# Shifted-window attention block with MLP, one core: both bands' scores and both bands' attend put together, with fixed PSUM banks for Q, K and V

## The chip, the cores and the metric

One Trainium2 chip, one of its cores. The metric is the device time of one execution in microseconds (us): the median of 3 runs for the kernel before. One further execution was profiled; all rows below are from it.

## The reference

A Swin transformer block over x of 32 images, 56 x 56 tokens, 128 channels, all in float32, window 7 x 7 (N = 49 tokens), shift 3, 4 heads of 32 channels:

```python
h = roll(layernorm(x, g1, b1), (-3, -3))              # 64 windows an image
q, k, v = split(windows(h) @ w_qkv + b_qkv)
attn = softmax((q * 32**-0.5) @ k.T + rel_bias + MASK)    # 49 x 49 for each window and head
x = x + roll(windows_back((attn @ v) @ w_proj + b_proj), (3, 3))
h2 = layernorm(x, g2, b2)
out = x + gelu(h2 @ w_fc1 + b_fc1) @ w_fc2 + b_fc2    # 128 -> 512 -> 128
```

## The kernel before

An image is cut into 4 steps of 14 rows, so there are 128 steps in all. A step has two bands of 7 rows; a band is 8 windows side by side, 392 tokens. The tokens of a step lie as 7 tiles of 112 (`HALVES`: a first half of 4 tiles, a second of 3).

The work is a software pipeline over steps, written out by hand as one `step(at)` for each engine, and each engine runs its list strictly in the order of the code. In the iteration of step s, with `at.has(d)` standing for step s+d, there run: statistics and normalisation of the input (`xn1`) for s+2; its transposes, Q and K for s+1; V, scores, softmax and attention for s; projection, residual, second layer norm and the first seven chunks of fc1/gelu for s-1; the last chunk, fc2 and the last addition for s-2. Semaphores order the engines; `wait(..., at.count(...))` waits for so many increments.

What runs where:

- TensorE (PE): `scores` (64 matmuls a band), `make_hidden` n = 0 to 7 (fc1 for one band and one chunk, three matmuls each), `project` (7 tiles, in two halves), `make_values`, `make_out` (fc2, two halves), `transpose_probs`, `transpose_x` and `transpose_x2` (two halves each), `attend` (64 matmuls a band), `make_q`, `make_k` (band 0 in plain float32, band 1 as three products).
- ScalarE (ACT): `gelu`, `exp`, and nearly all copies out of PSUM: `copy_v0`, `copy_probsT` (two instructions a band), `copy_x`, `copy_x2`, `copy_q`, `copy_k`, `copy_o`, and `round_x`. Exp and Gelu need different tables, so two table loads stand in a step: one ahead of the first exp, one at the `table_probe` line.
- VectorE (DVE): `shift_scores` (bias, maximum, subtraction), `inverse_sums`, statistics (`raw_stats`, `mean_var`), `normalise`, additions to the stream (`add_to_stream`; `add_mlp` is the last addition of layer two), `split_x`, `split_x2`, `copy_v1`.
- GpSimd (POOL): `normalise_probs`, the two reciprocal roots (`rstd1`, `rstd2`) and two additions of a bias row to the stream (signalled by `x1_biased` and `x_biased`).
- SyncE (SP) issues all loads (they wait for `x_biased`) and all stores (they wait for `out_added`).

PSUM has 8 banks: 0 to 3 for scores and transposed probabilities (two a band), 4 and 5 for Q, K, V and O in turn, 6 and 7 for whatever is indexed by tokens. `V_USE`, `Q_USE` and `K_USE` say which of banks 4 and 5 each band uses; O of one band fills 196 columns of both, one bank for each parity of the window.

The parts of TensorE's list that the change touches, in their order before: scores 0; hidden 7; project 0 and 1; values 0; scores 1; out 0; transpose_probs 0; out 1; transpose_x 0; attend 0; transpose_x2 0; transpose_x 1; values 1; transpose_x2 1; Q 0; hidden 0; K 0; hidden 1; transpose_probs 1; hidden 2 and 3; attend 1; hidden 4; Q 1; hidden 5; K 1; hidden 6. `make_q` of band 1 waits for O of band 1 to have been copied, since it writes the same bank:

```python
wait(pe, o_copied, at.count(2, band + 1))
qk_product(at, Q_USE[band], 0, band).then_inc(qk_made, 1)
```

Of the kernel before, what the change touches and what calls it, by code (L numbers as in the profile page):

```python
# [93 lines left out]
def swin_block(nc, x, g1, b1, w_qkv, b_qkv, w_proj, b_proj, rel_slices, g2, b2, w_fc1, b_fc1, w_fc2,  # L94
# [3 lines left out]
    with ExitStack() as ctx:  # L98
# [148 lines left out]

        V_USE, Q_USE, K_USE = (0, 0), (1, 0), (0, 1)

        def qkvo_psum(use):  # L250
            return psum[:, QKVO_BANK + use % 2, :]

        def o_psum(parity):
            return psum[:, QKVO_BANK + parity, 0:PAIRS * N]

# [9 lines left out]
        def v_copy(band):  # L265
            rows = HALF + N
            return (vs[0:rows, band, :, :].rearrange("m a c -> m (a c)"),
                    qkvo_psum(V_USE[band])[0:rows, :])

# [71 lines left out]
        def _(pool):  # L341
# [16 lines left out]

            def step(at):
                if at.has():  # L360
                    normalise_probs(at, 0)
# [11 lines left out]
                if at.has(2):  # L373

                    wait(pool, var1_ready, at.count(1, 1, 2))
                    pool.tensor_tensor(rstd1[:, :], ve1[:, :], minus_half[:, :], ALU.pow).then_inc(rstd1_ready, 1)  # L376
                if at.has(1):

                    wait(pool, x_loaded[at.slot(1)], dma_count(at.slot(1), at.image(1)))
                    wait(pool, xn1_ready, at.count(2, 2, 1))  # L380

                    if at.has(1 - STEPS):
                        wait(pool, out_stored[at.slot(1)], dma_count(at.slot(1), at.image(1 - STEPS)))
                    pool.tensor_tensor(stream[:, at.slot(1), :, :], x_in[:, at.slot(1), :, :],  # L384
                                       brow_proj[:, :].unsqueeze(1).to_broadcast([TOK, TILES, C]),
                                       ALU.add).then_inc(x_biased, 1)

# [3 lines left out]
        def _(act):  # L391
# [10 lines left out]

            def copy_probsT(at, band):
                for f in range(2):
                    wait(act, probsT_made, at.count(4, 2 * band + f + 1))
                    act.activation(probsT[:, band, f, :, :, :].rearrange("p a q n -> p (a q n)"),  # L406
                                   psum[:, S_BANK + 2 * band + f, :], ACT.Copy).then_inc(probsT_copied, 1)

            def copy_o(at, band):

                wait(act, o_made, at.count(2, band + 1))
                image = oT[:, :, band, :].rearrange("c i (a w j) -> c w a i j", w=2, j=WIN)
# [28 lines left out]
            def copy_q(at, band):  # L441
                wait(act, qk_made, at.count(4, 2 * band + 1, 1))
                for parity in range(2):
                    last = act.activation(qd[:, band, parity, :], qkvo_psum(Q_USE[band])[:, 0:BAND], ACT.Identity,  # L444
                                          bias=bias_q[:, parity:parity + 1], scale=parity_one[:, parity:parity + 1])
                last.then_inc(qk_copied, 1)

            def copy_k(at, band):
                wait(act, qk_made, at.count(4, 2 * band + 2, 1))
                act.activation(kT[:, band, :], qkvo_psum(K_USE[band])[:, 0:BAND], ACT.Identity,  # L450
                               bias=bias_k[:, :]).then_inc(qk_copied, 1)
# [11 lines left out]
            def step(at):  # L463
# [7 lines left out]
                if at.has(1):  # L471
                    copy_x(at, 0)
                if at.has():
                    copy_o(at, 0)
                if at.has(-1):
# [23 lines left out]
                if at.has():  # L499
                    copy_o(at, 1)  # L500
                if at.has(-1):
# [13 lines left out]
        def _(dve):  # L515
# [130 lines left out]
            def step(at):  # L646
# [58 lines left out]
        def _(pe):  # L705
# [34 lines left out]
            def transpose_probs(at, band):  # L740

                wait(pe, probs_normed, at.count(2, band + 1))
                for f in range(2):
                    for pair in range(PAIRS):
                        last = pe.transpose(psum[:, S_BANK + 2 * band + f, 128 * pair:128 * (pair + 1)],  # L745
                                            probs[:, band, f, 2 * pair:2 * pair + 2, :].rearrange("p w m -> p (w m)"),
                                            ident[:, :])
                    last.then_inc(probsT_made, 1)

            def attend(at, band):  # L750
                wait(pe, probsT_copied, at.count(4, 2 * band + 2))

                wait(pe, (v0_copied, v1_copied)[band], at.count(1, 1))

                if band == 0:
                    wait(pe, qk_copied, at.count(4, 4))
                elif at.has(1):
                    wait(pe, qk_copied, at.count(4, 2, 1))
                pe.sem_inc(attend_begun, 1)
                for pair in range(PAIRS):  # L760
                    for parity in range(2):
                        keys = slice(HALF * parity, HALF * parity + N)
                        for h in range(HEADS):
                            rows = slice(HD * h, HD * (h + 1))
                            last = pe.matmul(o_psum(parity)[rows, pair * N:(pair + 1) * N], vs[keys, band, pair, rows],
                                             probsT[keys, band, h // 2, pair, h % 2, 0:N], start=True, stop=True)
                last.then_inc(o_made, 1)
# [6 lines left out]

            def qk_product(at, use, part, band):
                if band == 0:

                    return pe.matmul(qkvo_psum(use)[:, 0:BAND], wqk[:, part, :], xT[:, at.slot(1) % 2, 0, :, 0:N],
                                     start=True, stop=True)
                return product(qkvo_psum(use)[:, 0:BAND], wqk_hi[:, part, :], wqk_lo[:, part, :],  # L780
                               xT_hi[:, :], xT_lo[:, :])

            def make_q(at, band):

                if band == 0:
                    wait(pe, xT_copied, at.count(2, 2, 1))
                else:
                    wait(pe, xT_split, at.count(1, 1, 1))

                wait(pe, o_copied, at.count(2, band + 1))  # L790
                qk_product(at, Q_USE[band], 0, band).then_inc(qk_made, 1)

            def make_k(at, band):

                if band == 0:
                    wait(pe, v1_copied, at.count(1, 1))
                else:
                    wait(pe, o_copied, at.count(2, 2))
                qk_product(at, K_USE[band], 1, band).then_inc(qk_made, 1)

            def make_values(at, band):

                if band == 0:
                    wait(pe, qk_copied, at.count(4, 3))
                else:
                    wait(pe, o_copied, at.count(2, 1))
                rows = HALF + N
                for pair in range(PAIRS):
                    windows = xT[:, at.slot() % 2, band, 2 * pair:2 * pair + 2, :].rearrange("c w n -> c (w n)")
                    last = pe.matmul(qkvo_psum(V_USE[band])[0:rows, pair * C:(pair + 1) * C], windows[:, 0:rows],  # L810
                                     wv[:, :], start=True, stop=True)
# [58 lines left out]
            def step(at):  # L870
                if at.has():
                    scores(at, 0)
                if at.has(-2):

                    make_hidden(at, 7, -2)
                if at.has(-1):

                    wait(pe, o_copied, at.count(2, 2, -1))
# [19 lines left out]
                if at.has(1):  # L898
                    transpose_x(at, 1)
                if at.has():  # L900
                    make_values(at, 1)
                if at.has(-1):
                    transpose_x2(at, 1)
# [13 lines left out]
                if at.has():  # L917
                    attend(at, 1)
                if at.has(-1):
# [70 lines left out]
```

## Time and profile before

| | |
|---|---|
| median of 3 runs | 3276.6 us (3276.32 to 3279.51) |
| the profiled execution | 3275.45 us, its span 3273.7 us |
| granted TensorE clock, mean | 0.999 of full |
| PE busy (matmul) | 3117.6 us, 95% |
| DVE busy | 2814.3 us, 86% |
| ACT busy | 2283.0 us, 70% |
| POOL busy | 1316.7 us, 40% |
| DMA | 111.95 MB, mean 34 GB/s |

The busy shares are averages over a loop that repeats 128 times. Matmuls are pipelined, so a busy TensorE is not one at its peak; the distance from the start of one group to the start of the next says more than the duration of one. With several engines near their limit, the question is which wait ends last at each hand-over inside one step.

### The profile page before, as it was taken

The page shows a single profiled execution, that of the slowest core. Times are in us where ns is not written, and L with a number is a line of the kernel's source. Part 1 is how long each engine was busy: PE and PEld are TensorE (multiplying, and loading weights), DVE is VectorE, ACT ScalarE, POOL GpSimd, SP SyncE. Part 2 cuts the span into 40 slices and gives each one's busy share as a digit, 9 for nine tenths or more (in the row PEclk, how much of TensorE's full clock was granted, in tenths as well). Part 3 has the DMA queues.
Part 4 walks back from the last instruction along what each step waited for, and adds up shares of the span by engine and source line. Part 5 has one row for each costly group of instructions (what it writes and reads, how often), then busy time and mean ns, then how long its engine had stood idle before and what let it go on. Part 6 is the DMA issues. An engine that isn't in the chain of part 4 may idle for free.

```text
span 3273.7 us, 121784 instructions
## 1 busy us (share of the span) xinstructions
PE 3117.6 (95%) x51984; PEld 2750.4 (84%) x51984; DVE 2814.3 (86%) x7463; ACT 2283.0 (70%) x4478; POOL 1316.7 (40%) x775
## 2 busy tenths in 40 slices
PE   5999999999999999999999999999999999999998
PEld 4888888888888888888888888888888888888887
DVE  6888888888888888888888888888888888888885
ACT  3667766776777677767776777677767776776675
POOL 2344434443444444344434443444344434443442
PEclk9999999999999999999999999999999999999999
DMA  1111111111111111111111111111111111111110
GB/s 51 34 32 37 36 33 32 37 37 32 32 36 37 32 34 35 37 32 36 33 37 32 36 32 37 32 37 32 37 32 37 34 35 32 37 34 34 32 27 22
DMA packets 217584, 111.95 MB, mean 34 GB/s; under 512 B 15094, under 2 KB 216790, under 8 KB 217046
## 3 DMA queue, kind: packets, MB, share of 16 engines
q1 hardware_dynamic: 216899, 104.14, 12.4%
q8 instruction: 413, 6.77, 0.9%
q14 instruction: 125, 1.02, 0.1%
q10 hardware_dynamic: 147, 0.02, 0.0%
HBM read 52.73 MB, written 51.38 MB: 32 GB/s over the span
## 4 chain that ended last, share of the span: by engine, by line
DVE 43%; ACT 30%; PE 16%; issue 10%; SPq 0%; POOL 0%; DMA 0%; DVEq 0%; POOLq 0%; ACTq 0%
DVE stream L620 9%; DVE scores L600 8%; DVE row_max L603 8%; ACT hT L460 7%; DVE xn L588 6%; DVE raw L566 5%; ACT L482 5%; ACT qd L444 4%; PE psum L771 4%; ACT probsT L406 4%; PE psum L729 4%; DVE row_sum L613 4%; PE psum L773 3%; PE psum L772 3%; ACT xT L425 2%
## 5 line engine op out<-in xcount | busy, mean ns | idle before, releaser
L858 PE MATMUL psum<-wfc,hT 128*112 128x128 f32 x7168 | 835.6, 274 | 1.0 <-ACT hT L460 0.7
L858 PEld LDWEIGHTS psum<-wfc,hT 128*112 128x112 f32 x7168 | 797.8, 177 | 8.3 <-ACT hT L460 1.0
L356 POOL TENSOR_TENSOR probs<-probs,row_inv 128x784 f32<-128x784 f32 x256 | 389.4, 1521 | 987.1 <-DVE row_inv L615 987.1
L460 ACT ACTIVATE hT<-psum,bias_h 128x392 f32<-128x392 f32 x1024 | 598.8, 605 | 71.1 <-PE psum L773 70.7
L406 ACT ACTIVATE probsT<-psum 128x512 f32<-128x512 f32 x512 | 281.5, 613 | 484.7 <-PE psum L745 484.7
L588 DVE TENSOR_SCALAR xn<-x_in,mean,rstd 112x128 f32<-112x128 f32 x896 | 466.0, 587 | 1.8 <-POOL rstd L376 1.7
L368 POOL TENSOR_TENSOR stream<-stream,brow_fc 112x896 f32<-112x896 f32 x128 | 267.3, 2088 | 485.6 <-DVE xn L588 485.6
L771 PE MATMUL psum<-x2T_hi,wfc_hi 128*128 128x392 f32 x1024 | 448.7, 438 | 2.6 <-DVE x2T_lo L638 1.5
L400 ACT ACTIVATE probs<-scores 128x784 f32<-128x784 f32 x256 | 224.0, 875 | 210.0 <-DVE scores L605 210.0
L444 ACT ACTIVATE qd<-psum,bias_q,parity_one 128x392 f32<-128x392 f32 x512 | 318.4, 674 | 59.0 <-PE psum L773 55.8
L773 PE MATMUL psum<-x2T_lo,wfc_hi 128*128 128x392 f32 x1024 | 348.5, 340 | 0.0
L772 PE MATMUL psum<-x2T_hi,wfc_lo 128*128 128x392 f32 x1024 | 347.9, 340 | 0.0
L376 POOL TENSOR_TENSOR rstd<-ve,minus_half 112x7 f32<-112x7 f32 x128 | 190.7, 1490 | 360.7 <-DVE ve L582 360.7
L600 DVE TENSOR_TENSOR scores<-psum,bias_rel 128x784 f32<-128x784 f32 x256 | 248.9, 972 | 92.7 <-PE psum L729 92.5
L620 DVE TENSOR_TENSOR stream<-psum,stream 112x512 f32<-112x512 f32 (+1 forms) x512 | 304.5, 615 | 20.9 <-PE psum L858 13.1
L736 PE MATMUL psum<-ident,xn 112*128 112x112 f32 x1792 | 269.1, 267 | 54.4 <-DVE stream L620 41.2
L771 PEld LDWEIGHTS psum<-x2T_hi,wfc_hi 128*128 128x128 f32 x1024 | 191.8, 187 | 138.9 <-DVE x2T_lo L638 76.2
L384 POOL TENSOR_TENSOR stream<-x_in,brow_proj 112x896 f32<-112x896 f32 x128 | 286.7, 2239 | 0.0
L745 PE MATMUL psum<-ident,probs 128*128 128x128 f32 x2048 | 267.1, 274 | 9.1 <-POOL probs L356 9.1
L736 PEld LDWEIGHTS psum<-ident,xn 112*128 112x128 f32 x1792 | 177.8, 141 | 106.4 <-issue 90.0
L810 PE MATMUL psum<-wv,xT 128*113 128x128 f32 x2048 | 266.2, 273 | 0.3 <-ACT oT L414 0.3
L605 DVE TENSOR_TENSOR scores<-scores,row_max 128x784 f32<-128x784 f32 x256 | 249.5, 975 | 8.7
(78 smaller groups left out, 5869.6 us busy)
## 6 DMA issues: line engine op xcount, KB each, us to landing
x_in<-in_x SPq DMA_DIRECT2D x224, 168.0 KB
out<-stream SPq DMA_DIRECT2D x224, 168.0 KB
x_in<-in_x SPq DMA_DIRECT2D x224, 17.5 KB
out<-stream SPq DMA_DIRECT2D x224, 17.5 KB
x_in<-in_x SPq DMA_DIRECT2D x224, 10.5 KB
out<-stream SPq DMA_DIRECT2D x224, 10.5 KB
x_in<-in_x SPq DMA_DIRECT2D x32, 96.0 KB
out<-stream SPq DMA_DIRECT2D x32, 96.0 KB
```

The costliest lines, as they stand in the source:

```text
L356: pool.tensor_tensor(p, p, r.unsqueeze(2).to_broadcast([128, 2 * WINDOWS, N]), ALU.mult).then_inc(probs_normed, 1)
L406: act.activation(probsT[:, band, f, :, :, :].rearrange("p a q n -> p (a q n)"), psum[:, S_BANK + 2 * band + f, :], ACT.Copy).then_inc(prob ...
L444: last = act.activation(qd[:, band, parity, :], qkvo_psum(Q_USE[band])[:, 0:BAND], ACT.Identity, bias=bias_q[:, parity:parity + 1], scale= ...
L460: act.activation(hT[:, chunk, band * BAND:(band + 1) * BAND], tok_psum(FC1 + n)[:, 0:BAND], ACT.Gelu, bias=bias_h[:, chunk:chunk + 1]).the ...
L588: last = dve.tensor_scalar(dst[:, t, :], src[:, t, :], mean[:, t:t + 1], rstd[:, t:t + 1], ALU.subtract, ALU.mult)
L600: dve.tensor_tensor(sc, scores_psum(band), bias_rel[:, last_band, :, :, :].rearrange("p f w m -> p f (w m)"), ALU.add).then_inc(scores_bia ...
L620: return dve.tensor_tensor(s, tok_psum(use)[0:TOK, 0:(t1 - t0) * C], s, ALU.add)
L736: last = pe.transpose(tok_psum(use)[:, (t - t0) * TOK:(t - t0 + 1) * TOK], src[:, t, :], ident[0:TOK, 0:TOK])
L771: pe.matmul(made, w_hi, x_hi, start=True, stop=False)
L772: pe.matmul(made, w_lo, x_hi, start=False, stop=False)
L773: return pe.matmul(made, w_hi, x_lo, start=False, stop=True)
L858: last = pe.matmul(tok_psum(FC2 + h)[0:TOK, (t - t0) * C:(t - t0 + 1) * C], hT[:, chunk, t * TOK:(t + 1) * TOK], wfc2[:, chunk, :], start= ...
```

## The change

- PE runs the scores of both bands at the head of the step, hidden 7 and the projections behind them.
- PE runs `attend` once, for both bands (128 matmuls), where attend 1 stood. O of both bands lies in the same two banks (392 columns each), and `copy_o` runs once, with two instructions of 392 columns where there were four of 196.
- Values 1 moves up, between transpose_x 0 and transpose_x 1; transpose_x2 0 and 1 stand together behind transpose_x 1.
- Q has bank 4, K has bank 5, V has 4 for band 0 and 5 for band 1; the waits follow.
- DVE's two `add_mlp` stand together, ahead of the normalisation of `xn2`.
- POOL's addition `x_biased` for s+1 moves from the end of an iteration to its beginning.
- `transpose_probs` reads 113 partitions in place of 128, and `copy_probsT` copies 4 x 113 columns in place of 512.

```diff
-        V_USE, Q_USE, K_USE = (0, 0), (1, 0), (0, 1)
+        V_BANK, Q_BANK, K_BANK = (0, 1), 0, 1
         def o_psum(parity):
-            return psum[:, QKVO_BANK + parity, 0:PAIRS * N]
+            return psum[:, QKVO_BANK + parity, 0:BANDS * PAIRS * N]
@@ gpsimd step
+                if at.has(1):
+                    wait(pool, x_loaded[at.slot(1)], dma_count(at.slot(1), at.image(1)))
+                    wait(pool, xn1_ready, at.count(2, 2, 1))
+                    if at.has(1 - STEPS):
+                        wait(pool, out_stored[at.slot(1)], dma_count(at.slot(1), at.image(1 - STEPS)))
+                    pool.tensor_tensor(stream[:, at.slot(1), :, :], x_in[:, at.slot(1), :, :],
+                                       brow_proj[:, :].unsqueeze(1).to_broadcast([TOK, TILES, C]),
+                                       ALU.add).then_inc(x_biased, 1)
                 if at.has():
                     normalise_probs(at, 0)
...
@@ scalar
-                act.activation(probsT[:, band, f, :, :, :].rearrange("p a q n -> p (a q n)"),
-                               psum[:, S_BANK + 2 * band + f, :], ACT.Copy).then_inc(probsT_copied, 1)
+                act.activation(probsT[:, band, f, :, :, :].rearrange("p a q n -> p a (q n)")[:, :, 0:rows],
+                               psum[:, S_BANK + 2 * band + f, :].rearrange("p (a n) -> p a n", a=PAIRS)[:, :, 0:rows],
+                               ACT.Copy).then_inc(probsT_copied, 1)
-            def copy_o(at, band):
-                wait(act, o_made, at.count(2, band + 1))
+            def copy_o(at):
+                wait(act, o_made, at.count(1, 1))
...
@@ vector step
                 if at.has(-2):
                     add_mlp(at, 0)
+                    add_mlp(at, 1)
                 if at.has(-1):
                     wait(dve, rstd2_ready, at.count(1, 1, -1))
                     wait(dve, x2T_made, at.count(2, 2, -2))
                     normalise(xn2, stream[:, at.slot(-1), :, :], mean2, rstd2, xn2_ready)
-                if at.has(-2):
-                    add_mlp(at, 1)
@@ tensor
-            def attend(at, band):
-                wait(pe, probsT_copied, at.count(4, 2 * band + 2))
-                wait(pe, (v0_copied, v1_copied)[band], at.count(1, 1))
-                if band == 0:
-                    wait(pe, qk_copied, at.count(4, 4))
-                elif at.has(1):
-                    wait(pe, qk_copied, at.count(4, 2, 1))
+            def attend(at):
+                wait(pe, probsT_copied, at.count(4, 4))
+                wait(pe, v0_copied, at.count(1, 1))
+                wait(pe, v1_copied, at.count(1, 1))
+                if at.has(1):
+                    wait(pe, qk_copied, at.count(4, 2, 1))
...
             def make_q(at, band):
                 if band == 0:
                     wait(pe, xT_copied, at.count(2, 2, 1))
+                    wait(pe, v0_copied, at.count(1, 1))
                 else:
                     wait(pe, xT_split, at.count(1, 1, 1))
-                wait(pe, o_copied, at.count(2, band + 1))
+                    wait(pe, o_copied, at.count(1, 1))
@@ tensor step
                 if at.has():
                     scores(at, 0)
+                    scores(at, 1)
                 if at.has(-2):
                     make_hidden(at, 7, -2)
                 if at.has(-1):
                     project(at, 0)
                     project(at, 1)
                 if at.has():
                     make_values(at, 0)
-                    scores(at, 1)
...
                 if at.has(1):
                     transpose_x(at, 0)
                 if at.has():
-                    attend(at, 0)
+                    make_values(at, 1)
+                if at.has(1):
+                    transpose_x(at, 1)
                 if at.has(-1):
                     transpose_x2(at, 0)
-                if at.has(1):
-                    transpose_x(at, 1)
-                if at.has():
-                    make_values(at, 1)
-                if at.has(-1):
                     transpose_x2(at, 1)
...
                 if at.has():
-                    attend(at, 1)
+                    attend(at)
```

## Rows read from the trace of the kernel before

**Rows 1.** Windows, one step: length, then busy time (instructions) of each engine.

```profile
1513.03:1538.16 25.13, 24.27 (x408) 21.43 (x407) 21.91 (x60) 17.85 (x36) 10.28 (x6) 1.00 0.13 34
```

**Rows 2.** Timeline, PE, that step: start us, length us, line, operation [idle before, releaser].

```profile
1513.03 0.95 PE L729 MATMUL psum<-kT,qd 64*49 64x49 f32 x64
1513.91 0.44 PE L771 MATMUL psum<-x2T_hi,wfc_hi 128*128 128x392 f32 x1
...
1525.17 0.57 PE L736 MATMUL psum<-ident,xn 112*128 112x112 f32 x4
1525.68 0.81 PE L765 MATMUL psum<-probsT,vs 49*32 49x49 f32 x64
1526.53 0.57 PE L736 MATMUL psum<-ident,xn 112*128 112x112 f32 x4
1527.43 0.48 PE L736 MATMUL psum<-ident,xn 112*128 112x112 f32 x3 [0.32 <-DVE stream L620]
1527.74 1.04 PE L810 MATMUL psum<-wv,xT 128*113 128x128 f32 x8
1528.62 0.47 PE L736 MATMUL psum<-ident,xn 112*128 112x112 f32 x3
...
1534.01 0.80 PE L765 MATMUL psum<-probsT,vs 49*32 49x49 f32 x64 [0.26 <-ACT probsT L406]
...
1535.84 0.42 PE L771 MATMUL psum<-xT_hi,wqk_hi 128*128 128x392 f32 x1 [0.23 <-ACT oT L414]
...
1538.16 0.95 PE L729 MATMUL psum<-kT,qd 64*49 64x49 f32 x64
```

**Rows 3.** Timeline, ACT, same step.

```profile
1514.75 0.59 ACT L460 ACTIVATE hT<-psum,bias_h 128x392 f32<-128x392 f32 x1 [0.54 <-PE psum L773]
1515.36 1.28 ACT L400 ACT_TABLE_LOAD   x1
1517.07 0.87 ACT L400 ACTIVATE probs<-scores 128x784 f32<-128x784 f32 x1 [0.43 <-DVE scores L605]
...
1527.94 0.52 ACT L425 ACTIVATE xT<-psum 128x168 f32<-128x168 f32 x2 [0.26 <-PE psum L736]
...
1532.75 1.11 ACT L406 ACTIVATE probsT<-psum 128x512 f32<-128x512 f32 x2
...
1535.06 0.63 ACT L414 ACTIVATE oT<-psum 128x196 f32<-128x196 f32 x2
...
1538.27 0.59 ACT L450 ACTIVATE kT<-psum,bias_k 128x392 f32<-128x392 f32 x1
```

**Rows 4.** Timeline, DVE, same step and the head of the next.

```profile
1518.02 0.96 DVE L613 TENSOR_REDUCE row_sum<-probs 128x16 f32<-128x784 f32 x1
...
1524.34 0.68 DVE L620 TENSOR_TENSOR stream<-psum,stream 112x512 f32<-112x512 f32 x1
1524.94 1.88 DVE L588 TENSOR_SCALAR xn<-stream,mean,rstd 112x128 f32<-112x128 f32 x7
1526.73 0.55 DVE L620 TENSOR_TENSOR stream<-psum,stream 112x384 f32<-112x384 f32 x1
...
1534.80 3.67 DVE L588 TENSOR_SCALAR xn<-x_in,mean,rstd 112x128 f32<-112x128 f32 x7
1539.17 0.97 DVE L600 TENSOR_TENSOR scores<-psum,bias_rel 128x784 f32<-128x784 f32 x1 [0.71 <-PE psum L729]
```

**Rows 5.** Timeline, POOL, same step: the addition that signals x_biased.

```profile
1534.60 2.25 POOL L384 TENSOR_TENSOR stream<-x_in,brow_proj 112x896 f32<-112x896 f32 x1
```

**Rows 6.** Groups by line and form: busy us, mean ns, idle before.

```profile
L406 ACT ACTIVATE probsT<-psum 128x512 f32<-128x512 f32 x512 | 281.5, 613 | 484.7 <-PE psum L745 484.7
L414 ACT ACTIVATE oT<-psum 128x196 f32<-128x196 f32 x512 | 154.5, 380 | 18.0 <-PE psum L765 1.4
```

**Rows 7.** Timeline, SP's queue: the stores of one step.

```profile
1527.31 2.25 SPq L310 DMA_DIRECT2D out<-stream  x6
```

**Rows 8.** Windows: as rows 1, then clock, DMA share, GB/s.

```profile
1530.50:1531.50 1.00, 1.00 (x5) 0.59 (x4) 1.00 (x5) 1.00 (x3) 0.00 (x0) 1.00 0.05 13
```

More of the change, by code:

```diff
@@ L267, in v_copy @@
             return (vs[0:rows, band, :, :].rearrange("m a c -> m (a c)"),
-                    qkvo_psum(V_USE[band])[0:rows, :])
+                    qkvo_psum(V_BANK[band])[0:rows, :])
         def token_pieces(s, dram, img, tile):
@@ L443, in copy_q @@
                 for parity in range(2):
-                    last = act.activation(qd[:, band, parity, :], qkvo_psum(Q_USE[band])[:, 0:BAND], ACT.Identity,
+                    last = act.activation(qd[:, band, parity, :], qkvo_psum(Q_BANK)[:, 0:BAND], ACT.Identity,
                                           bias=bias_q[:, parity:parity + 1], scale=parity_one[:, parity:parity + 1])
@@ L758, in attend @@
                     wait(pe, qk_copied, at.count(4, 2, 1))
                 pe.sem_inc(attend_begun, 1)
[L760 to L766, printed above, removed]
+                for band in range(BANDS):
+                    for pair in range(PAIRS):
+                        cols = slice((band * PAIRS + pair) * N, (band * PAIRS + pair + 1) * N)
+                        for parity in range(2):
+                            keys = slice(HALF * parity, HALF * parity + N)
+                            for h in range(HEADS):
+                                rows = slice(HD * h, HD * (h + 1))
+                                last = pe.matmul(o_psum(parity)[rows, cols], vs[keys, band, pair, rows],
+                                                 probsT[keys, band, h // 2, pair, h % 2, 0:N], start=True, stop=True)
@@ L773, in product, with qk_product @@
                 return pe.matmul(made, w_hi, x_lo, start=False, stop=True)
-            def qk_product(at, use, part, band):
+            def qk_product(at, bank, part, band):
                 if band == 0:
-                    return pe.matmul(qkvo_psum(use)[:, 0:BAND], wqk[:, part, :], xT[:, at.slot(1) % 2, 0, :, 0:N],
+                    return pe.matmul(qkvo_psum(bank)[:, 0:BAND], wqk[:, part, :], xT[:, at.slot(1) % 2, 0, :, 0:N],
                                      start=True, stop=True)
-                return product(qkvo_psum(use)[:, 0:BAND], wqk_hi[:, part, :], wqk_lo[:, part, :],
+                return product(qkvo_psum(bank)[:, 0:BAND], wqk_hi[:, part, :], wqk_lo[:, part, :],
                                xT_hi[:, :], xT_lo[:, :])
@@ L797, in make_k @@
                 else:
-                    wait(pe, o_copied, at.count(2, 2))
-                qk_product(at, K_USE[band], 1, band).then_inc(qk_made, 1)
+                    wait(pe, o_copied, at.count(1, 1))
+                qk_product(at, K_BANK, 1, band).then_inc(qk_made, 1)
             def make_values(at, band):
[L803 to L806, printed above, removed]
+                wait(pe, qk_copied, at.count(4, 3 + band))
                 rows = HALF + N
@@ L809, in make_values @@
                     windows = xT[:, at.slot() % 2, band, 2 * pair:2 * pair + 2, :].rearrange("c w n -> c (w n)")
-                    last = pe.matmul(qkvo_psum(V_USE[band])[0:rows, pair * C:(pair + 1) * C], windows[:, 0:rows],
+                    last = pe.matmul(qkvo_psum(V_BANK[band])[0:rows, pair * C:(pair + 1) * C], windows[:, 0:rows],
                                      wv[:, :], start=True, stop=True)
@@ L876, in step @@
                 if at.has(-1):
-                    wait(pe, o_copied, at.count(2, 2, -1))
+                    wait(pe, o_copied, at.count(1, 1, -1))
                     project(at, 0)
```

30 lines of the change are left out of this document (11 added, 19 removed).

## The prediction

> **What bounds the kernel now.** I read the page first (PE 95% busy, DVE 86%, ACT 70%, POOL 40%), then a window of one step, then the chain of waits in order of time, and last the timeline of each engine over that step. The loop is strictly periodic. From the first scores of one step to those of the next are 25.13 us [rows 1, 2], and 128 such steps make 3216.6 of the span of 3273.7 us; prologue and epilogue are the other 57. So one question decides: by how much does the period change, times 128.
>
> No single engine sets the period. PE has only 0.81 us of marked idle time in a step: 0.32 ahead of the second half of transpose_x, 0.26 ahead of attend 1, 0.23 ahead of Q 1 [rows 2]. The other 24.32 us are its own work, a floor that the change does not lower, since it removes no matmul. DVE waits 0.71 us for the first scores of the next step [rows 4]. The chain of waits shows one loop through three engines, and the reader should follow it, for the sum is made along it. In times relative to the step's first scores (1513.03 is 0.00):
>
> - DVE shifts scores 0 (starts 1.02 after them), adds the projection, and takes the sums of band 0 at 4.99, just after exp 0 ended at 4.91 [rows 3, 4]. It works on without a gap to add_mlp 0 (11.31), xn2 (11.91) and add_mlp 1 (13.70, ends 14.25) [rows 4].
> - That addition releases transpose_x 1 on PE (14.40), that copy_x 1 on ACT (14.91), and behind it stands the table load for Gelu (15.43) [rows 2, 3].
> - ACT then has no idle time up to the end of copy_o 1: probsT 1 at 19.72, copy_o 1 from 22.03 to 22.66 [rows 3].
> - That releases Q 1 on PE (22.81), and from Q 1 through hidden 5, K 1 and hidden 6 it is 2.32 us to the next scores at 25.13 [rows 2].
>
> A thing saved beside this loop is worth nothing; each delay on it is paid 128 times.
>
> **The change part by part.**
>
> *Attend for both bands at the end.* PE's total is the same, but 64 matmuls that ran at 12.65, off the loop, now stand between probsT 1 and copy_o, on it. A band takes 0.85 us by the distance to the next group at the first place; at the second its row says 0.80 [rows 2]. Before, copy_o 1 started 1.05 after attend 1, and ACT came to it without idle time. With 128 matmuls the end comes 0.84 (the distance from attend 0 until ACT could copy, which its 0.85 of work makes a lower bound) plus 0.85 after the start, 1.69. Addition: 1.69 - 1.05 = +0.64; bounds 0.60 and 0.68, the doubt being a few hundredths at each end. ACT could use that time, but its list has nothing that it may take: copy_o stands behind gelu 3, and gelu 4 and everything else stand behind copy_o. On PE only hidden 4 stands between attend and Q 1, so PE waits as well.
>
> *copy_o for both bands.* Before, two instructions of 196 columns took 0.63 us and Q 1 began 0.15 later. The 392-column copy is not in the trace. 512 columns take 613 ns and 196 take 380 [rows 6], so 0.74 ns a column, and 392 take about 525 ns. Two of them, overlapping as before (0.63 against 2 x 0.38, 0.13 saved), take 0.92: +0.29. Bounds: +0.25 if the short copies' cost is mostly fixed, +0.33. The copy_o 0 that disappears (0.57 us, at about 13.5) saves nothing on the loop: ACT waits 0.26 us for copy_x 1 right behind that place [rows 3], and it will wait there again.
>
> *probsT with 452 columns.* 60 columns fewer by 0.74 are 0.04 us an instruction, two of them on the loop; -0.1 with what the clipped pattern saves at the end, bounds -0.12 and 0. The transposes of 113 partitions save nothing that I count.
>
> *Both scores at the head.* Scores take 0.88 us of PE (1513.03 to 1513.91) [rows 2]. Scores 1 moves ahead of hidden 7, so hidden 7 is 0.88 later, and so is gelu 7, which started at 1.72. Queued behind gelu 7 on ACT is the table load, and behind that exp 0. gelu 7 to table load is 0.61, the load 1.28 [rows 3]. Exp 0 can then start at 1.72 + 0.88 + 0.61 + 1.28 = 4.49 in place of 4.04, since only 0.43 of the 0.88 was idle time ahead of exp 0 [rows 3]. The sums of band 0 on DVE follow exp 0 by less than 0.1, so DVE is 0.42 late from there on, through the second shift to add_mlp 0. That DVE list has no idle time to give it back. Bounds: 0 and 0.47.
>
> *Projections 0.88 later.* Hidden 7 starts at 1.76 and takes about 0.58 (a quarter of the 2.32 above); the 14 instructions of the projections, by the 0.88 that values 1 takes for 8, take 1.5. So the first half is done at about 3.2 and the second at 3.9, and DVE, through with the first shift at 3.9, adds them at 3.9 and 4.5. Covered; it would cost what they are late. Values 0 keeps its place (two groups changed sides), and its copy is followed by idle time on ACT.
>
> *The order in the middle.* add_mlp 0 ends 0.42 later, which releases transpose_x 0 at 12.56 in place of 12.14. Then values 1 (0.88 by the distance to the next group), transpose_x 1 from 13.95 (0.31), transpose_x2 0 from 14.26 [rows 2]. add_mlp 1 ends by 12.9, so it is no longer what is waited for: the 0.32 wait goes. But ACT copies x2 0 ahead of x 1 (its list is not changed there), so copy_x 1 now stands behind transpose_x2 0. ACT starts the copy of x2 0 about 0.61 after that transpose, 14.87; then 0.43, then copy_x 1's 0.52 [rows 3], and the table load starts at 15.82 in place of 15.43: +0.39. The step is no better for the earlier addition: what was won is taken by values 1 and by that order. On PE the second half of transpose_x2 has to wait for copy_x 1 in the same bank, a new wait of about 1.1 us, in time that before held attend 0 and values 1.
>
> *xn2 behind both additions.* It starts at about 12.8 in place of 11.9. Its first four tiles are ready at 13.9, ahead of their transpose at 14.26; its end (14.7) delays POOL's bias addition and normalise_probs 1 to about 18.4, ahead of transpose_probs 1 at 18.9. Covered, by half a microsecond.
>
> *x_biased at the head of POOL's list.* Before, this addition of 2.25 us ran beside DVE's normalisation of xn1, which took 3.67 us in place of xn2's 1.88 for as many instructions [rows 4, 5]. Now it waits for xn1 to be done and runs behind it: 1.79 us come off DVE, but off the loop, where DVE then waits for scores. Gain: 0, and 2.5 us of idle time instead of 0.71. The moved step carries a wait for the stores of a step 3 back. Those are issued at 14.28, and 4.2 us later next to nothing moves [rows 7, 8]; now they are issued near 13 and wanted near 24. Covered. The loads on SP now come earlier, right behind the stores; DVE wants them a step later.
>
> The SBUF page of the Trainium skill (State Buffer, section on the two sides) says that GpSimd and a VectorE instruction in a two-port mode, or with two SBUF inputs, exclude each other for a whole instruction. By that rule the trace agrees: 3.67 against 1.88. By the rule the moved addition could also block the third part of the first shift, which is a rival below.
>
> **The sum.** 0.39 (late table load) - 0.10 (probsT) + 0.64 (attend) + 0.29 (copy_o) = +1.22 us a step. Q 1 moves from 22.81 to 24.03, and the period from 25.13 to 26.35. Times 128: +156 us. On the profiled execution's 3275.5 that is 3432 us; on the median, 1.1 above it, 3433 us, 4.8% slower.
>
> **Rivals.**
>
> - *Exp 0's delay is absorbed* (15%). If the table load starts sooner behind gelu 7, or DVE's sums had more room, the 0.39 falls to nothing: period +0.83, 106 us, 3383 us. For it: only 0.42 to 0.45 reach DVE and such margins are small. Against it: exp 0 has no other way around the load.
> - *PE at its floor* (6%, faster). The waits on PE vanish: 25.13 - 0.81 = 24.32 us, 3276.6 - 104 = 3173 us. The place is Q 1: it decides if attend and copy_o end before hidden 4 does, that is, if hidden 4's 0.8 us (1.83 from attend 1 to Q 1, less 0.80 and the wait of 0.23) cover them. For it: DVE has 1.79 us more, and transpose_x 1 is free sooner. Against it: the copy of O alone is 0.92 and starts only when attend ends.
> - *Nothing measurable* (4%). The loop loses about 1.2 us and gets it back from the xn1 normalisation. That needs DVE's tail to be on the loop; it waited 0.71 us there [rows 4].
> - *POOL's addition is late and holds up what stands behind it* (4%). If the stores were late, or if it ran into the subtraction of the first shift (third of three operations of 0.97), up to its 2.25 us would be added: 3433 + 288 = 3720 us. By its wait it should start near 24.1 and end near 26.4, about 3 us ahead of that subtraction.
> - *Further hand-overs bind* (6%): scores 1 now needs the copy of K 1, which gelu 5 and Q 1's copies precede on ACT. Some 0.3 us more a step: about 3471 us.
>
> The forecast itself has 65%. Its own bounds are 0 - 0.12 + 0.60 + 0.25 = +0.73 and 0.44 - 0 + 0.68 + 0.33 = +1.45 a step: 3370 to 3462. To take in the last rival the range goes to 3475. Faster by over 0.2% (about what a measurement of this kernel tells from no change) 6%, within it 4%, slower 90%.
>
> **What would show it.** A period of 26.3 to 26.4 us. ACT idle about 1.4 us ahead of gelu 7 (0.54 before), none ahead of exp 0; a new wait of DVE's sums of band 0 for exp of about 0.4; a wait of some 1.1 us on PE for ACT's xT copy; ACT idle about 0.6 us ahead of copy_o, PE idle about 0.3 behind hidden 4, released by oT; xn1 at 1.88 us, and DVE's wait for the first scores near 2.5 or more. Wrong would be: the forecast of the size if Q 1 is released by something other than oT, or if exp 0 is still released by DVE; of the sign if PE's waits in a step sum to less than 0.8 us.

## The result and the profile after

The changed kernel took 3439.5 us, the median of 4 runs (3432.8 to 3444.5), against 3278.1 us (3276.3 to 3280.1): ratio 1.0491, 95% interval 1.0471 to 1.0511. The forecast was 3433 us. The total agrees to 0.2%, but only partly for the reasons given: the usual step grew by less than forecast, and a second cause that the forecast did not have made up the difference. That the two cancel is luck.

The timeline of PE in the changed kernel, from one head of a step to the next; columns as in [rows 2]:

```profile
1505.38 1.80 PE L728 MATMUL psum<-kT,qd 64*49 64x49 f32 x128
1507.11 0.44 PE L771 MATMUL psum<-x2T_hi,wfc_hi 128*128 128x392 f32 x1
...
1517.92 0.57 PE L735 MATMUL psum<-ident,xn 112*128 112x112 f32 x4 [0.64 <-DVE stream L620]
1518.33 1.04 PE L809 MATMUL psum<-wv,xT 128*113 128x128 f32 x8
1519.21 0.84 PE L735 MATMUL psum<-ident,xn 112*128 112x112 f32 x7
1521.18 0.48 PE L735 MATMUL psum<-ident,xn 112*128 112x112 f32 x3 [1.14 <-ACT xT L427]
...
1526.49 1.37 PE L765 MATMUL psum<-probsT,vs 49*32 49x49 f32 x128 [0.16 <-ACT probsT L407]
1527.79 0.45 PE L771 MATMUL psum<-x2T_hi,wfc_hi 128*128 128x392 f32 x1
...
1528.97 0.42 PE L771 MATMUL psum<-xT_hi,wqk_hi 128*128 128x392 f32 x1 [0.38 <-ACT oT L416]
...
1531.27 1.81 PE L728 MATMUL psum<-kT,qd 64*49 64x49 f32 x128
```

The period is 25.89 us (25.13 before). The marked waits sum to 2.32 us in place of 0.81, and the two new ones fit the forecast's account: 0.64 ahead of transpose_x 0, for add_mlp 0 (the forecast named that releaser, not a length), and 1.14 ahead of the second half of transpose_x2, for copy_x 1 (1.1 in the forecast). ACT in the same step, against [rows 3]:

```profile
1507.95 0.59 ACT L462 ACTIVATE hT<-psum,bias_h 128x392 f32<-128x392 f32 x1 [1.39 <-PE psum L773]
1508.56 1.28 ACT L400 ACT_TABLE_LOAD   x1
1509.85 0.87 ACT L400 ACTIVATE probs<-scores 128x784 f32<-128x784 f32 x1
...
1520.08 0.54 ACT L440 ACTIVATE x2T_hi<-psum 128x448 fp32r<-128x448 f32 x1 [0.94 <-PE psum L735]
1520.52 0.52 ACT L427 ACTIVATE xT<-psum 128x168 f32<-128x168 f32 x2
1521.06 1.28 ACT L482 ACT_TABLE_LOAD   x1
...
1525.32 1.02 ACT L407 ACTIVATE probsT<-psum 128x452 f32<-128x452 f32 x2
...
1527.90 0.93 ACT L416 ACTIVATE oT<-psum 128x392 f32<-128x392 f32 x2 [0.18 <-PE psum L765]
```

The late gelu 7 shows as 1.39 us of idle time, and no idle time is left between the table load and exp 0. DVE, against [rows 4], pays 0.30 us ahead of the sums and has 3.14 us to spare for the next scores; xn1 runs at 1.88 us:

```profile
1510.76 0.97 DVE L613 TENSOR_REDUCE row_sum<-probs 128x16 f32<-128x784 f32 x1 [0.30 <-ACT probs L400]
...
1527.27 1.88 DVE L588 TENSOR_SCALAR xn<-x_in,mean,rstd 112x128 f32<-112x128 f32 x7
1532.29 0.97 DVE L600 TENSOR_TENSOR scores<-psum,bias_rel 128x784 f32<-128x784 f32 x1 [3.14 <-PE psum L728]
```

But 127 periods that are 0.775 longer make only 98 us, and the span grew by 163.3. Most of the rest is in the distances between successive starts of rstd2 on POOL, which mark equal points of successive steps. There are 127; the first and the last, in which the pipeline fills and drains, are left out here. Before, 123 of 125 are within 0.1 us of 25.12. After, 96 are within 0.1 of 25.90, and 29 are longer, by up to 4.5 us, 55 us in sum. What happens in such a step stands in PE's timeline:

```profile
498.05 1.31 PE L765 MATMUL psum<-probsT,vs 49*32 49x49 f32 x121 [0.16 <-ACT probsT L407]
501.54 0.38 PE L765 MATMUL psum<-probsT,vs 49*32 49x49 f32 x7 [2.19 <-issue]
501.85 0.69 PE L771 MATMUL psum<-x2T_hi,wfc_hi 128*128 128x392 f32 x1
502.35 0.53 PE L772 MATMUL psum<-x2T_hi,wfc_lo 128*128 128x392 f32 x1
```

In the middle of the merged attend, 7 matmuls from its end, PE stands still for 2.19 us. "issue" says that no engine and no transfer of data is seen to hold it up. Afterwards a product that takes 0.34 takes 0.53, up to the next scores. Windows over another such step show what that is (start and end, length, then busy time of PE, PE loads, DVE, ACT, POOL, then clock, DMA share, GB/s):

```profile
3028.50:3029.00 0.50, 0.00 (x0) 0.00 (x0) 0.50 (x3) 0.00 (x0) 0.00 (x0) 1.00 0.00 0
3029.50:3030.00 0.50, 0.50 (x8) 0.43 (x8) 0.35 (x2) 0.15 (x1) 0.01 (x1) 1.00 0.00 0
3031.00:3031.50 0.50, 0.50 (x2) 0.50 (x3) 0.00 (x0) 0.38 (x1) 0.50 (x1) 0.50 0.00 0
3033.50:3034.00 0.50, 0.50 (x5) 0.50 (x4) 0.00 (x0) 0.50 (x3) 0.00 (x0) 0.96 0.00 0
```

The gap (3028.49 to 3029.50) comes at full clock with the data transfers silent; less than a microsecond after PE resumes the granted clock is 0.50 (1.2 GHz in place of 2.4), for about 3 us. Inside the loop the clock of the changed kernel falls ten times, each time 1.1 to 4.4 us behind the start of such a gap; before, it does not fall in the loop at all. So the clock is a consequence of the gap, not its cause.

The DMA view of the first of these two steps shows what arrives in the gap (queue and kind, then packets, MB, share of 16 engines; window 499.2 to 500.2), and the windows show it too: 33 GB/s over half a microsecond are 16 KB, and nothing else starts between 498.6 and 501.6.

```profile
q8 instruction: 1, 0.02, 5.9%
499.00:499.50 0.50, 0.35 (x39) 0.23 (x24) 0.50 (x3) 0.27 (x1) 0.00 (x0) 1.00 0.12 33
500.00:500.50 0.50, 0.00 (x0) 0.00 (x0) 0.50 (x3) 0.00 (x0) 0.00 (x0) 1.00 0.00 0
```

It is a packet of 16384 bytes of PE's instructions, which starts at 499.22 and lands at 500.16. PE stops at 499.35 and goes on at 501.54, 1.38 us behind the landing. What is left of the growth, 163.3 - 98 - 54 (the 55 less 1 before) = some 11 us, lies in the first steps and the last.

### The profile page after: what moved, and what is told of

Read it like the earlier page. It is cut to its first block, busy times and chain, and to the rows that moved or that the text cites. A ratio compares the mean times of both kernels' runs of the same rounds, so it can differ in the third digit from the quotient of the medians.

```text
span 3437.0 us, 121273 instructions
## 1 busy us (share of the span) xinstructions
PE 3063.7 (89%) x51984; PEld 2734.4 (80%) x51984; DVE 2603.5 (76%) x7463; ACT 2224.4 (65%) x4222; POOL 1304.7 (38%) x775
## 4 chain that ended last, share of the span: by engine, by line
ACT 34%; PE 34%; DVE 22%; issue 9%; SPq 0%; DMA 0%; POOL 0%; DVEq 0%; POOLq 0%; ACTq 0%
PE psum L728 7%; PE psum L771 5%; PE psum L765 5%; DVE raw L566 5%; PE psum L735 5%; ACT L482 5%; ACT L400 5%; ACT qd L446 4%; PE psum L773 4%; PE psum L772 4%; DVE scores L600 4%; DVE row_max L603 4%; ACT hT L462 4%; DVE row_sum L613 4%; ACT oT L416 3%
## 5 line engine op out<-in xcount | busy, mean ns | idle before, releaser
L857 PE MATMUL psum<-wfc,hT 128*112 128x128 f32 x7168 | 824.9, 273 | 1.0 <-ACT hT L462 0.7
L407 ACT ACTIVATE probsT<-psum 128x452 f32<-128x452 f32 x512 | 257.2, 567 | 400.1 <-PE psum L745 400.1
L771 PE MATMUL psum<-x2T_hi,wfc_hi 128*128 128x392 f32 x1024 | 457.4, 447 | 2.5 <-DVE x2T_lo L638 2.2
L735 PE MATMUL psum<-ident,xn 112*128 112x112 f32 x1792 | 243.6, 264 | 233.2 <-ACT xT L427 145.9
L367 POOL TENSOR_TENSOR stream<-x_in,brow_proj 112x896 f32<-112x896 f32 x128 | 272.9, 2132 | 272.2 <-issue 258.5
L620 DVE TENSOR_TENSOR stream<-psum,stream 112x512 f32<-112x512 f32 (+1 forms) x512 | 295.0, 615 | 33.8 <-PE psum L857 17.1
L613 DVE TENSOR_REDUCE row_sum<-probs 128x16 f32<-128x784 f32 x256 | 246.6, 963 | 47.4 <-ACT probs L400 47.4
L603 DVE TENSOR_REDUCE row_max<-scores 128x16 f32<-128x784 f32 x256 | 248.3, 970 | 8.7
```

Of the source, the lines that this page charges most:

```text
L603: dve.tensor_reduce(mx, rows, AX_X, ALU.max).then_inc(max_done, 1)
L613: dve.tensor_reduce(s, p, AX_X, ALU.add).then_inc(sum_done, 1)
L735: last = pe.transpose(tok_psum(use)[:, (t - t0) * TOK:(t - t0 + 1) * TOK], src[:, t, :], ident[0:TOK, 0:TOK])
L771: pe.matmul(made, w_hi, x_hi, start=True, stop=False)
L857: last = pe.matmul(tok_psum(FC2 + h)[0:TOK, (t - t0) * C:(t - t0 + 1) * C], hT[:, chunk, t * TOK:(t + 1) * TOK], wfc2[:, chunk, :], start= ...
```

## The experiments

Theory A: the gaps come from the supply of instructions to PE when very many small ones follow each other. Theory B: they come from PE's new waits, through its clock. The other runs size the forecast's terms. Periods are medians over the 127 distances; excess is the sum of what those over 0.1 us longer have above that, first and last left out. Each run's ratio is to runs of the kernel before made beside it, whose medians are the first row.

| run | median us | ratio to before, 95% interval | period | excess |
|---|---|---|---|---|
| before | 3276 to 3280 | 1 | 25.12 | 1 |
| changed | 3439.5 | 1.0491 (1.0471 to 1.0511) | 25.90 | 55 |
| e1_attend_split | 3411.5 | 1.0406 (1.0391 to 1.0422) | 25.87 | 36 |
| e2_scores_apart | 3395.1 | 1.0347 (1.0329 to 1.0366) | 25.68 | 28 |
| e3_both_apart | 3368.0 | 1.0267 (1.0250 to 1.0285) | 25.64 | 21 |
| e4_attend_twice | 3366.2 | 1.0263 (1.0248 to 1.0278) | 25.43 | 44 |
| e5_pool_first | 3277.5 | 0.9995 (0.9986 to 1.0004) | 25.12 | 1 |
| e6_clipped | 3267.5 | 0.9963 (0.9950 to 0.9977) | 25.03 | 1 |
| e7_scores_together | 3337.8 | 1.0185 (1.0170 to 1.0200) | 25.55 | 7 |
| e8_aligned_4 | 3353.9 | 1.0227 (1.0213 to 1.0241) | 25.68 | 0.7 |
| e9_aligned_36 | 3459.2 | 1.0551 (1.0537 to 1.0566) | 25.68 | 101 |
| e10_mlp_together | 3295.1 | 1.0056 (1.0039 to 1.0073) | 25.22 | 1 |
| e11_early_table | 3223.0 | 0.9837 (0.9822 to 0.9852) | 24.67 | 1 |

**e1: the changed kernel, attend in two bursts.**

```diff
                 if at.has(-1):
                     make_hidden(at, 2)
+                if at.has():
+                    attend(at, 0)
+                if at.has(-1):
                     make_hidden(at, 3)
                 if at.has():
-                    attend(at)
+                    attend(at, 1)
```

> The changed kernel with attend cut in two again: band 0 runs ahead of hidden 3, band 1 where the merged attend stood, copy_o still once for both. Theory A (the irregular long steps come from the supply of instructions to PE when very many small matmuls run back to back): the long steps at the attend vanish (about 44 of the 55 us in excess of the usual period), those at the 128 scores stay (about 11 us); the usual period falls from 25.90 by the 0.36 us that the second band's attend put between probsT and copy_o, to 25.5; in all about 3437 - 44 - 46 = 3347 us. Theory B (the long steps come from the new waits on PE, through its clock): the waits on PE are not fewer, so the long steps stay, about 3391 us.

Both theories' numbers failed. The period did not fall: PE had waited only 0.16 us for probsT ahead of the merged attend, so 64 matmuls put in front of that place delay the other 64 by as much. Attend 1 starts 1.69 us after probsT 1 does, where the merged attend of the changed kernel starts 1.17 after it, and ACT reaches copy_o no sooner. The 13 gaps at the attend became shorter (0.8 to 1.4 us in place of mostly 2) but did not vanish; all lie in the last 7 matmuls of the second burst, with six instructions (hidden 3 and its loads) between the bursts. So theory A in this form, that bursts of 64 are free of gaps, is wrong. Shorter gaps, up to 0.5 us, stayed in the 128 scores.

```profile
1542.80 0.77 PE L766 MATMUL psum<-probsT,vs 49*32 49x49 f32 x60
1544.45 0.28 PE L766 MATMUL psum<-probsT,vs 49*32 49x49 f32 x4 [0.88 <-issue]
```

**e2: the changed kernel, scores 1 back behind values 0.**

> The changed kernel with the scores of band 1 back behind values 0. The price of the late exp 0 was forecast at 0.39 us a step and reads 0.25 in the trace of the changed kernel: the usual period falls from 25.90 to 25.65 and the wait of DVE's sums for exp 0 goes. Theory A (instruction supply in bursts): the irregular gaps inside the scores go too (about 11 us in all), those at the attend stay (44 us): 3437 - 32 - 11 = 3394 us. Theory B (PE's waits and its clock): no change in the long steps, 3405 us.

The period fell by 0.22 and the gaps inside the scores went; all that are left are in or right behind the attend. That is for A, and for the size read in the trace.

**e3: both.**

> The changed kernel with both: attend in two bursts of 64 matmuls, scores in two bursts of 64. Theory A (instruction supply): no irregular long step is left, period 25.9 - 0.36 - 0.25 = 25.3, about 3437 - 55 - 78 = 3304 us. Theory B (PE's waits and clock): PE keeps its 1.1 us wait for copy_x 1, so some long steps stay, above 3340 us.

25.64: the attend cut in two gives next to nothing, the scores apart give what they gave in e2. A's time (3304) and its promise that no long step is left both failed, for the reasons of e1; 13 gaps of 0.7 to 1.3 us stay at the attend. 3368 us is above 3340, as B had it, so this run does not speak against B; e4, e8 and e9 do.

**e4: the kernel before, attend 1 done twice over.** The order and PE's waits are those of before.

```diff
-                for pair in range(PAIRS):
+                for pair in [p for again in range(band + 1) for p in range(PAIRS)]:
```

> The kernel before, in which attend 1 does its 64 matmuls twice over (same operands, same result), and nothing else. It puts the price of 64 more attend matmuls between probsT 1 and copy_o by itself. The forecast's working says +0.64 to +0.85 us a step (25.13 to 25.8 or 26.0); the trace of the changed kernel says 64 more add about 0.4 to 0.5 to the burst, and about +0.4 to the period: 25.5. Theory A (instruction supply): some 15 irregular long steps appear with a gap inside or right behind the attend, 30 to 45 us in all, about 3275 + 50 + 40 = 3365 us. Theory B (they come from PE's new waits in the changed kernel): none appear, since the order and the waits are those of before, about 3325 us.

```profile
1601.96 1.37 PE L765 MATMUL psum<-probsT,vs 49*32 49x49 f32 x128 [0.26 <-ACT probsT L406]
1603.26 0.45 PE L771 MATMUL psum<-x2T_hi,wfc_hi 128*128 128x392 f32 x1
```

3366 us where A said 3365 and B 3325 (the period rose by less than A took, 0.3 for 0.4, and the excess is at the upper end of its 30 to 45): the 15 gaps appear, most of them of 1.4 to 2.4 us. B is out. The 64 further matmuls cost 0.50 us (1.30 from start to the next group, against a length of 0.80) and 0.30 in the period; the forecast priced them at 0.85 and 0.64.

**e8 and e9: the count of instructions.** A became exact when the gaps of the changed kernel were numbered by iteration. The gap moves through the attend: 7 matmuls left at iteration 17, 3 left at 26, just behind it at 35 and 44, and 7 left again at 49, 81 and 113. Nine iterations move it 8 instructions later (a matmul and its weight load are two), 32 iterations bring it back. Both hold if an iteration has 824 PE instructions (408 matmuls, 408 loads, and 8 more, which would be those that only order things) and the gap lies at a multiple of 256: 9 x 824 is 8 short of a multiple of 256, 32 x 824 is one. In e4, with 128 more, the gap moves 2 later in 11 iterations, which makes 954 an iteration: 408 + 408 + 128, and 10 others. The profile pages count PE's instructions in another way: before, 413 packets of queue q8 carry 6.77 MB, 16.4 KB each, which for twice 51984 matmuls and the 8 to 10 others of each iteration is some 254 instructions a packet. e4 has 64 matmuls with their loads more in each of 128 steps, 16384 instructions, and 477 packets: 64 more, so 256 a packet. So two kernels were made from e2, which differ in one number:

```diff
+                if at.has():
+                    for _ in range(8):
+                        pe.sem_inc(attend_begun, 1)
                 if at.has(-1):
                     transpose_x2(at, 1)
...
+            for _ in range(4):          # 36 in e9
+                pe.sem_inc(attend_begun, 1)
             run_steps(pe, images, step)
```

> The kernel of e2_scores_apart with 8 semaphore increments added to PE's list in each iteration, ahead of the second half of transpose_x2 where PE waits 1.1 us anyway, and 4 once ahead of the loop. Theory A, made exact: the gaps come where the count of PE instructions crosses a multiple of 256 near the end of the attend burst. All 12 gaps of e2 lie in iterations s where 824 s modulo 256 is 160 to 184. With 832 instructions an iteration the crossing takes only four places, and with 4 ahead they are 12, 76, 140 and 204 on that scale: none in the bad range. So no long step at all is left: e2's 3395 less 27 = about 3368 us. Theory B (waits and clock) and a theory of chance collisions with transfers: the long steps stay as in e2, 3395 us.

> The same as e8_aligned_4, but with 36 semaphore increments once ahead of the loop in place of 4, and nothing else. Theory A: the four places are 44, 108, 172 and 236, of which 172 is in the bad range, so every fourth step is long, 32 of them by about 2.2 to 3.5 us: 3368 + 70 to 110 = 3438 to 3478 us. Theory B and chance collisions: no difference to e8 (3395 us both).

32 semaphore increments, issued once ahead of the loop, are worth 105 us: 3353.9 against 3459.2. e8 is 14 us under its forecast, which took e2's median of 3395 less the 27 us of a profiled execution that was itself 12 us under that median. It has no gap in the loop (one is left in the last iteration, whose count differs); e9 has one in every fourth iteration, 2, 6, 10 to 126, always at the same instruction, the first behind the attend:

```profile
1912.69 0.50 PE L771 MATMUL psum<-x2T_hi,wfc_hi 128*128 128x392 f32 x1 [2.44 <-issue]
1913.00 0.53 PE L772 MATMUL psum<-x2T_hi,wfc_lo 128*128 128x392 f32 x1
```

By the code, work, waits and transfers are the same in both. That settles A in its exact form, for place and count. The traces show the fetch too: over all runs, behind the first 60 us, each of the 125 gaps of more than 0.28 us that are put down to issue ends 1.2 to 1.8 us (median 1.4) behind the landing of a 16384-byte packet on q8, whether the gap is 0.3 us long or 2.6. What happens in that 1.4 us no row shows.

**e5: the kernel before, x_biased at the head of POOL's list.**

> The kernel before with one edit: POOL's addition x_biased for s+1 moves from the end of an iteration to its beginning. The forecast's term: DVE's normalisation of xn1 falls from 3.67 to 1.88 us, its wait for the next scores grows from 0.71 to 2.5, and the time does not move: within 0.1% of 3278. Rival: some of DVE's end is on the loop after all, up to 1.79 us a step: then 1 to 6% faster.

No difference within 0.14%, the lower end of the interval. The trace shows the whole of what DVE gains being waited away, against 3.67 and 0.71 in [rows 4]:

```profile
1535.12 1.88 DVE L588 TENSOR_SCALAR xn<-x_in,mean,rstd 112x128 f32<-112x128 f32 x7
1539.48 0.97 DVE L600 TENSOR_TENSOR scores<-psum,bias_rel 128x784 f32<-128x784 f32 x1 [2.48 <-PE psum L729]
```

**e6: the kernel before, probsT clipped to 4 x 113 columns.**

> The kernel before with one edit: transposes of 113 partitions and probsT copies of 4 x 113 columns. The forecast's term is -0.10 us a step, 13 us less (3265); the changed kernel's trace suggests -0.09. Rival: other work fills in behind the copies and nothing is gained (3278).

0.37% faster, 25.03: the term was 0.10 and is 0.09. The copy's mean falls from 613 ns [rows 6] to 567:

```profile
L407 ACT ACTIVATE probsT<-psum 128x452 f32<-128x452 f32 x512 | 257.4, 567 | 477.7 <-PE psum L748 477.7
```

**e7: the kernel before, both scores at the head.**

> The kernel before with one edit: both bands' scores at the head of PE's step. The forecast's term was a late exp 0 that costs 0.39 us a step; the changed kernel's trace suggests 0.25. So the usual period goes from 25.12 to 25.4 or 25.5 (+32 to +50 us), with a wait of DVE's sums for exp of about 0.3. Theory A (a multiple of 256 instructions inside a burst) adds short gaps in the scores, some 10 to 15 us in all: 3320 to 3340 us. Rival: the delay of exp 0 is absorbed, 3280 us.

25.55, +0.42: by itself the late exp 0 costs what the forecast said (0.39), and the wait ahead of the sums is 0.32. The excess is 7 us, with gaps of 0.2 to 0.5.

**e10: the kernel before, both add_mlp together.**

> The kernel before with one edit: DVE's two add_mlp together, ahead of xn2. PE's 0.32 us wait for the second addition goes, but transpose_x2 0, which stands ahead of transpose_x 1 on PE, now waits for xn2 (13.9 in place of 13.5). Forecast: nothing gained, 0 to +0.1 us a step, 3278 to 3290 us. Rival: the wait of 0.32 is really saved, 3278 - 41 = 3237 us.

0.56% slower, against the rival. The period, 25.22, is at the dear end of what was expected; the time is 19 us longer, past the 12 that were the upper bound, the other 6 us lying outside the usual steps. PE's wait did not go, it changed its releaser, from the addition to xn2, and grew from 0.32 to 0.48:

```profile
1510.07 0.89 PE L735 MATMUL psum<-ident,xn 112*128 112x112 f32 x7 [0.48 <-DVE xn L588]
```

**e11: an order that uses the early addition.** The kernel before with e5, e6 and e10, and four moves:

```diff
@@ PE
+                if at.has(1):
+                    transpose_x(at, 1)
                 if at.has(-1):
                     transpose_x2(at, 0)
-                if at.has(1):
-                    transpose_x(at, 1)
...
                     make_q(at, 0)
+                    make_k(at, 0)
                 if at.has(-1):
                     make_hidden(at, 0)
@@ ACT
-                if at.has(-1):
-                    copy_x2(at, 0)
                 if at.has(1):
                     copy_x(at, 1)
                 if at.has(-1):
...
                     act.activation(table_probe[:, :], bias_h[:, 0:1], ACT.Gelu).then_inc(gelu_loaded, 1)
+                    copy_x2(at, 0)
                     copy_x2(at, 1)
@@ DVE: copy_v1 ahead of split_x2 0
```

> A version meant to beat both: the kernel before with attend, scores and banks left as they are; the clipped probsT copies, x_biased at the head, both add_mlp together, and then an order that makes use of the early addition: transpose_x 1 ahead of transpose_x2 0 on PE, copy_x 1 and the Gelu table load ahead of copy_x2 0 on ACT, copy_v1 ahead of the splits on DVE, K 0 ahead of hidden 0 on PE. The load starts about 0.8 us sooner, 0.43 of it goes to copy_x2 0 behind it: -0.3 to -0.4 us, with -0.09 of the clipped copies 24.7 us a step, 3278 - 50 = 3228 us (range 3205 to 3260). Floor of PE's own work: 24.3 us a step, 3176 us. Rival: hidden 0, now behind the load, becomes the bound and nothing is gained (3267, the clipped copies alone).

3223.0 us, 1.63% faster than before; period 24.67 against a forecast of 24.7. ACT now goes from copy_o 0 to copy_x 1 to the load without a gap, and copies both halves of x2 behind it:

```profile
1501.54 0.57 ACT L416 ACTIVATE oT<-psum 128x196 f32<-128x196 f32 x2
1501.99 0.52 ACT L427 ACTIVATE xT<-psum 128x168 f32<-128x168 f32 x2
1502.53 1.28 ACT L482 ACT_TABLE_LOAD   x1
...
1503.93 0.87 ACT L440 ACTIVATE x2T_hi<-psum 128x448 fp32r<-128x448 f32 x2
```

PE's marked waits are down to 0.17 and 0.23 us a step.

## Why the prediction was right, and where it was not

**The loop and its links: right.** Each wait that was named along the chain is there: gelu 7 1.39 us (forecast 1.4), PE ahead of transpose_x2's second half 1.14 (1.1), PE ahead of Q 1 0.38 (0.3), DVE ahead of the sums 0.30 (0.4). transpose_x 0 starts at 12.54 (12.56). ACT's wait for the merged attend is 0.18 and was forecast at 0.6: that is the mis-sized term.

**The terms.** From the rows after, relative to 1505.38: the Gelu load starts at 15.68 (15.43 before), attend at 21.11 (20.98), copy_o at 22.52 (22.03), Q 1 at 23.59 (22.81).

- Late table load: +0.25, forecast 0.39. The late exp 0 is right by itself (e7: 0.42), and e2 gives 0.22 back when it is undone. In the changed kernel transpose_x 0 and values 1 follow each other more closely than was taken: 0.41 us from the one to the other, where the forecast used 0.51 from [rows 2]. That is 0.10 of the 0.14.
- probsT: -0.12 from load to attend, e6 -0.09; forecast -0.10. Right.
- Attend: 1.41 us from its start to copy_o, in place of 1.05: +0.36, forecast +0.64. This is the term that was mis-sized, outside its own bounds (0.60 and 0.68). The forecast took a second burst of 64 at the full 0.85; e4 measures it at 0.50. By the two lengths, 0.80 for 64 and 1.30 for 128, a matmul costs 7.8 ns and a burst 0.3 us once (an estimate from two points).
- copy_o: 1.07 us from its start to Q 1, in place of 0.78: +0.29, as forecast. The 392-column copy takes 524 ns where the slope of [rows 6] gave 525:

```profile
L416 ACT ACTIVATE oT<-psum 128x392 f32<-128x392 f32 x256 | 119.0, 524 | 44.2 <-PE psum L765 44.2
```

The sum is +0.78 where the forecast had +1.22, nearly at the lower end of its own bounds (0.73 to 1.45): 98 us in place of 156.

**What hid the miss.** 54 us of gaps in 29 steps, for which nothing was in the sum. It counted what 64 more small matmuls cost when they run, not what 256 PE instructions in 1.3 us ask of whatever supplies them. No row of before showed such a gap, since its bursts were half as long. The unforeseen 54 us and the over-priced 58 us nearly cancel, and that the forecast is right to 0.2% is luck. Without the gaps the time would be some 3385 us, still inside the range. As a sum it was right in sign and in two of four terms; the late table load was 0.14 us too dear, inside its bounds, and attend 0.28, outside them.

**At nothing, rightly.** x_biased (e5). The trace agrees with the rule that the prediction cites from the Trainium skill, that GpSimd and such a VectorE instruction exclude each other: apart, the seven instructions take 1.88 us, in the changed kernel and in e5; overlapped, they took 3.67. Of these the first took 2.13 us and ended 0.08 us after POOL's addition, and the other six took 0.33 each, as they do apart. The rival in which the moved addition blocks the shift did not occur.

**Both additions together** were costed at nothing won; e10 shows that alone they cost 0.10 us a step, and e11 that the early addition is worth something once the copy and the table load behind it move up with it.

## What to carry to other kernels

Price a merger by where it stands on the loop, not by its total: here 64 matmuls moved from a place beside the loop to a place on it, and 1.79 us a step that came off VectorE bought nothing. When many tiny instructions are put together on one engine, look at the distances between equal points of successive steps, not only at a typical step: a long step in four or five is invisible in a window of one. If an engine stands still on "issue", look for an instruction packet in the DMA view and number the instructions: gaps that stay at multiples of one count point to the supply, and a few instructions more or less tell it for sure.

## What the runs showed of the hardware

PE can run out of instructions. In a burst of 128 small matmuls with their loads (256 instructions in 1.3 us, 5 ns each) it stands still if a multiple of 256 instructions falls near the end of the burst or just behind it. In the changed kernel that is where 824 times the iteration is 160 to 184 modulo 256: all 16 such iterations of the loop have a gap, of 0.4 to 2.3 us, more than half of them of about 2. In e2 14 of the same 16 have one; in e9 there are 32, of 2.0 to 2.6. With the same count in about 2.2 us (e1, e3: two bursts of 64 with a product between) the gap is 0.7 to 1.4 us, in the scores (1.73 us for 256) 0.3 to 1.1, and at the kernel before's bursts of 64 none is seen. Each gap ends 1.2 to 1.8 us behind the landing of the 16384 bytes; the packet itself takes about 1.

The clock makes the gap cost more than its length. In e9 the gaps are 2.2 us on average. Behind 30 of the 32 the granted clock is at its lower level, for about 3 us mostly, and those steps are 2.9 to 4.7 us too long; the two steps in which the clock stays are 1.5 and 1.7 us too long.

The Trainium skill (Runtime: NRT & Kernel Launch, section on instruction fetch) says that instructions come in blocks of 16 KiB, 256 of them, and that crossing into a new block is mostly hidden. The count of 256 agrees with the places of the gaps in the changed kernel, e4, e8 and e9 and with e4's 64 further packets. That it is mostly hidden holds for the kernel before, where no gap is seen, and not for bursts such as these: 105 us between e8 and e9.
